# Order of the first loads, a layer norm over latents with its statistics as rows, and two tiles turned ahead of the expert stage's first product

## Time and profile before

| | |
|---|---|
| Median of 3 timed runs | 3268.74 us (3267.42 to 3273.45) |
| Profiled execution, own time | 3266.73 us |
| Its span, first to last instruction | 3264.7 us |
| PE busy | 2824.3 us, 87% |
| DVE, ACT, POOL busy | 57%, 49%, 21% |
| Granted TensorE clock, mean | 0.924 of full speed |

### The profile page before, as it was taken

One profiled execution on the slowest core, in us unless ns is written; L12 is line 12 of the kernel. 1 busy time (PEld: TensorE's weight loads), 2 busy tenths in 40 slices (PEclk: granted clock), 3 DMA queues, 4 the chain that ended last, 5 costly groups with the idle time before them and its releaser, 6 DMA issues. The chain is left out here.

```text
span 3264.7 us, 53416 instructions
## 1 busy us (share of the span) xinstructions
PE 2824.3 (87%) x18536; PEld 1728.8 (53%) x18537; DVE 1866.7 (57%) x4567; ACT 1584.1 (49%) x4331; POOL 678.6 (21%) x756
## 2 busy tenths in 40 slices
PE   7778988659999998679889999999988879959993
PEld 4635653425555555346555553455633455659992
DVE  5645765548787775758566642266423547743334
ACT  5425963227777774851246432154421539813331
POOL 3120021112112110112036520066300003301113
PEclk9878999679999999889999999999999989969996
DMA  1000020200000001000010010000000000141112
GB/s 71 3 15 5 2 85 0 71 0 1 2 2 1 2 2 63 1 14 2 17 41 1 1 64 0 7 1 1 1 29 13 7 23 2 79 170 37 35 33 83
DMA packets 36130, 80.64 MB, mean 25 GB/s; under 512 B 9089, under 2 KB 24530, under 8 KB 32050
## 3 DMA queue, kind: packets, MB, share of 16 engines
q1 hardware_dynamic: 30962, 64.68, 5.5%
q0 software_dynamic: 4368, 11.93, 1.3%
q10 hardware_dynamic: 560, 0.93, 0.1%
HBM read 63.18 MB, written 14.02 MB: 24 GB/s over the span
## 5 line engine op out<-in xcount | busy, mean ns | idle before, releaser
L2562 ACT ACTIVATE scores<-scores,min 128x128 f32<-128x128 f32 (+7 forms) x256 | 198.5, 775 | 86.7 <-DVE min L2545 82.6
L2543 DVE TENSOR_SCALAR zero_marks<-psum 128x128 f32<-128x128 f32 (+7 forms) x256 | 192.1, 750 | 67.8 <-PE psum L2475 65.9
L2545 DVE CUSTOM_DVE_ANT_0 scores<-psum,zero_marks 128x128 f32<-128x128 f32 (+7 forms) x256 | 194.1, 758 | 29.9 <-issue 0.9
L2482 PE MATMUL psum<-ident,scores 128*128 128x128 f32 x1152 | 172.9, 277 | 16.6 <-ACT probsT L2579 13.7
L2579 ACT ACTIVATE probsT<-psum 128x128 f32<-128x128 f32 (+7 forms) x256 | 163.0, 637 | 32.1 <-PE psum L2482 31.6
L4006 PE MATMUL psum<-Hn,W 128*128 128x512 f32 x384 | 169.9, 606 | 7.6 <-PEq L54 7.6
L1701 ACT ACTIVATE XT<-psum,early_weights 128x128 f32<-128x128 f32 x312 | 89.0, 368 | 176.2 <-PE psum L1621 176.2
L1621 PE MATMUL psum<-early_weights,XT 128*128 128x128 f32 x1248 | 150.8, 280 | 6.1 <-issue 3.2
L2482 PEld LDWEIGHTS psum<-ident,scores 128*128 128x128 f32 x1152 | 123.3, 141 | 55.9 <-issue 30.3
L1621 PEld LDWEIGHTS psum<-early_weights,XT 128*128 128x128 f32 x1248 | 145.9, 195 | 13.0 <-issue 11.9
L3854 POOL TENSOR_TENSOR probs<-probs,stat 128x512 f32<-128x512 f32 (+1 forms) x128 | 123.2, 986 | 99.6 <-DVE stat L3818 97.0
(11 more groups left out here) (628 smaller groups left out, 6728.5 us busy)
## 6 DMA issues: line engine op xcount, KB each, us to landing
W<-in_L3f_W SPq DMA_DIRECT2D x16, 1024.0 KB, 13.1
L3f_y_rows<-early_weights SPq DMA_DIRECT2D x39, 128.0 KB, 1.7
early_weights<-in_L2f_Wqkv SPq DMA_DIRECT2D x2, 1536.0 KB
W<-in_L2f_W SPq DMA_DIRECT2D x2, 1536.0 KB
XT<-in_xT SPq DMA_DIRECT2D x1, 2048.0 KB, 10.1
Xtok<-in_xtok SPq DMA_DIRECT2D x1, 2048.0 KB
L0f_rows<-Xtok SPq DMA_DIRECT2D x4, 512.0 KB, 2.9
W<-in_L0f_W SPq DMA_DIRECT2D x2, 1024.0 KB
```

The costliest lines, as they stand in the source:

```text
L2482: ins = pe.transpose(turned[:, kt * P:(kt + 1) * P], Sc[:, i % ROT, kt * P:(kt + 1) * P], K.ident[:])
L2543: dve.tensor_scalar(zero[:, i % 2, 0:n], sc(i)[:, 0:n], 0.0, -NEG, ALU.is_equal, ALU.mult)
L2545: dve.tensor_tensor_reduce(Sc[:, i % ROT, 0:n], sc(i)[:, 0:n], zero[:, i % 2, 0:n], 1.0, -NEG, ALU.add, ALU.min, low[:, i % ROT:i % ROT + ...
L2562: act.activation(p, p, ACT.Exp, bias=low[:, i % ROT:i % ROT + 1], scale=-1.0, accum_out=sums[:, u % 2, h:h + 1]).then_inc(s["exp_done"], 1)
```

## The change

Four places are edited.

1. In `setup`, SP waits for x and the first weights ahead of issuing the context and the token-major x, no longer behind it, and ACT issues its three loads in reverse order (cw, Wb, W).
2. `feature_ln` is replaced by `latent_ln`, with its statistics as rows: all 4 means first, then the sums of squares of both groups and all blocks into 8 rows of one bank, one root and one reciprocal on 8 x 512 values, then 4 products that spread the rows back over the partitions. The latents are worked on in place. POOL prepares two small matrices and clears a buffer in the same phase. It takes nine semaphores, the old one seven.
3. In the expert stage TensorE turns tile 1 ahead of up 0, and DVE does weights 0 ahead of x_out 0. The loop is the same.
4. In `L0_ffn` the phase of `block_mean` is gone; POOL's next phase begins with a memset of J to 1/128.

```diff
         @block.sync
         def _(sp):
             sp.dma_start(K.XT[0][:], w["xT"]).then_inc(s["loaded"], 16)
+            sp.wait_ge(s["loaded"], 16 * (1 + len(K.ahead)))
             sp.dma_start(K.ctxT[:], w["ctxT"]).then_inc(K.late, 16)
             sp.dma_start(K.Xtok[:], w["xtok"]).then_inc(K.late, 16)
-            sp.wait_ge(s["loaded"], 16 * (1 + len(K.ahead)))
...
-            for dst, src in K.ahead:
+            for dst, src in K.ahead[::-1]:
                 act.dma_start(dst, src).then_inc(s["loaded"], 16)
...
                 turn_x(0, 0)
+                turn_x(0, 1)
                 up(0, 0)
-                turn_x(0, 1)
...
-                x_out(0, 0)
                 dve.wait_ge(weights_in, 16 * (2 * EXPERTS + 1))
                 weights(0, 0)
+                x_out(0, 0)
                 x_out(0, 1)
                 weights(0, 1)
...
+def latent_ln(nc, K, J, src, g, b):
+    GROUPS_ = P // LAT
+    R = NB * GROUPS_
...
+        @block.gpsimd
+        def _(pool):
+            pool.memset(std[:], 0.0).then_inc(s["prepared"], 1)
+            pool.memset(wide[:], 0.0).then_inc(s["prepared"], 1)
+            pool.wait_ge(s["prepared"], 2)
+            pool.tensor_copy(wide[:, GROUPS_ * (NB - 1):GROUPS_ * NB], J.rearrange("p (g d) -> p g d", g=GROUPS_)[:, :, 0]).then_inc(s["prepared"], 1)
+            pool.tensor_copy(pick[:].rearrange("p j (g d) -> p (j g) d", g=GROUPS_), inner(K.ident[:, 0:R], LAT)).then_inc(s["prepared"], 1)
         @block.tensor
         def _(pe):
+            for j in range(NB):
+                pe.matmul(K.bank[j][:], J, src(j), start=True, stop=True).then_inc(s["mean_done"], 1)
+            pe.wait_ge(s["prepared"], 4)
+            for j in range(NB):
                 pe.wait_ge(s["squared"], j + 1)
+                at = GROUPS_ * (NB - 1 - j)
+                pe.matmul(K.bank[4][0:R, :], wide[:, at:at + R], sq[:, j % 2, :], start=(j == 0), stop=(j == NB - 1)).then_inc(s["var_done"], 1)
+            pe.wait_ge(s["recip_done"], 1)
+            for j in range(NB):
+                pe.wait_ge(s["centred"], j + 1)
+                pe.matmul(K.bank[j][:], pick[:, j, :], std[:], start=True, stop=True).then_inc(s["spread"], 1)
         @block.vector
         def _(dve):
+            for j in range(NB):
                 dve.wait_ge(s["mean_done"], j + 1)
+                dve.tensor_tensor(src(j), src(j), K.bank[j][:], ALU.subtract).then_inc(s["centred"], 1)
+            dve.wait_ge(s["std_done"], 1)
+            dve.reciprocal(std[0:R, :], std[0:R, :]).then_inc(s["recip_done"], 1)
+            for j in range(NB):
+                dve.wait_ge(s["spread"], j + 1)
+                dve.tensor_tensor(src(j), src(j), K.bank[j][:], ALU.mult).then_inc(s["normed"], 1)
         @block.scalar
         def _(act):
+            for j in range(NB):
                 act.wait_ge(s["centred"], j + 1)
                 if j >= 2:
                     act.wait_ge(s["var_done"], j - 1)
+                act.activation(sq[:, j % 2, :], src(j), ACT.Square).then_inc(s["squared"], 1)
+            act.wait_ge(s["var_done"], NB)
+            act.wait_ge(s["prepared"], 1)
+            act.activation(std[0:R, :], K.bank[4][0:R, :], ACT.Sqrt, bias=K.eps[0:R, 0:1]).then_inc(s["std_done"], 1)
+            for j in range(NB):
                 act.wait_ge(s["normed"], j + 1)
+                act.activation(src(j), src(j), ACT.Identity, scale=g, bias=b)
...
-                feature_ln(nc, K, J[:], NB, 1, lambda j, h: cb(j), lambda j, h: cb(j), lambda j: g[:], lambda j: b[:])
+                latent_ln(nc, K, J[:], cb, g[:], b[:])
...
-            block_mean(nc, K, J[:], P)
...
                 @block.gpsimd
                 def _(pool):
+                    pool.memset(J[:], 1.0 / P)
                     pool.iota(ordi[:], pattern=[[1, PICKED]], base=1, channel_multiplier=0).then_inc(s["counted"], 1)
```

More of the change, by code:

```diff
@@ L2160, in _ @@
             pool.affine_select(out=v, in_=v, compare_op=ALU.is_ge, fill=0.0, base=size - 1, pattern=[[size, n], [0, size]], channel_multiplier=-1)
[L2163 to L2169, removed]
+def latent_ln(nc, K, J, src, g, b):
+    GROUPS_ = P // LAT
+    R = NB * GROUPS_
+    names = "prepared mean_done centred squared var_done std_done recip_done spread normed"
+    with ExitStack() as es, phase(nc, K.sems, names) as (block, s):
+        sq = sbuf(es, nc, "squares", [P, 2, BLK])
+        std = sbuf(es, nc, "std", [P, BLK])
+        wide = sbuf(es, nc, "averaging_columns", [P, (2 * NB - 1) * GROUPS_])
+        pick = sbuf(es, nc, "row_picks", [P, NB, P])
+        @block.gpsimd
[5 more added lines that the diff above has]
+            pool.tensor_copy(pick[:].rearrange("p j (g d) -> p (j g) d", g=GROUPS_), inner(K.ident[:, 0:R], LAT)).then_inc(s["prepared"], 1)
@@ L2171, in _ @@
         @block.tensor
         def _(pe):
[L2173 to L2182, removed]
-                pe.wait_ge(s["squared"], j + 1)
[L2184 to L2188, removed]
+            for j in range(NB):
+                pe.matmul(K.bank[j][:], J, src(j), start=True, stop=True).then_inc(s["mean_done"], 1)
@@ L2190, in _ @@
         @block.vector
         def _(dve):
-            def centre(j):
+            for j in range(NB):
                 dve.wait_ge(s["mean_done"], j + 1)
[L2194 to L2208, removed]
+                dve.tensor_tensor(src(j), src(j), K.bank[j][:], ALU.subtract).then_inc(s["centred"], 1)
@@ L2210, in _ @@
+            dve.wait_ge(s["std_done"], 1)
[3 more added lines that the diff above has]
+                dve.tensor_tensor(src(j), src(j), K.bank[j][:], ALU.mult).then_inc(s["normed"], 1)
         @block.scalar
         def _(act):
-            def square(j):
+            for j in range(NB):
                 act.wait_ge(s["centred"], j + 1)
@@ L2215, in square @@
                     act.wait_ge(s["var_done"], j - 1)
[L2216 to L2222, removed]
-                act.wait_ge(s["var_done"], j + 1)
-                if j >= 2:
-                    act.wait_ge(s["normed"], j - 1)
-                act.activation(std[:, j % 2, :], K.bank[2 + j % 2][:], ACT.Sqrt, bias=K.eps[:, 0:1]).then_inc(s["std_done"], 1)
+                act.activation(sq[:, j % 2, :], src(j), ACT.Square).then_inc(s["squared"], 1)
[3 more added lines that the diff above has]
+            for j in range(NB):
                 act.wait_ge(s["normed"], j + 1)
-                for h in range(halves_):
-                    ins = act.activation(dst(j, h), xc[:, j % 2, h, :], ACT.Identity, scale=g(j)[:, h:h + 1], bias=b(j)[:, h:h + 1])
-                ins.then_inc(s["out"], 1)
+                act.activation(src(j), src(j), ACT.Identity, scale=g, bias=b)
 def feature_ln_rows(nc, K, J, n, halves_, src, dst, g, b, late=()):
```

## The result

The changed kernel took **3246.78 us** in the median of 4 runs (3245.30 to 3250.36), against 3268.62 for the kernel before on the same occasion (3267.42 to 3273.45). The ratio is 0.9932, interval 0.9918 to 0.9945: 21.8 us less, where 18.9 were forecast. The span of the profiled execution fell from 3264.7 to 3243.3 us, that is by 21.4; the mean granted clock rose from 0.924 to 0.928.

A forecast was written before the change was run, and what follows sets the result against it. The prediction took one chain of barrier-closed phases to bound the kernel, so the last-ending wait counts at each place. Gains 5.5 + 1.25 + 8.7 + 3.45 = 18.9 us off 3268.7 gave 3249.8, range 3241 to 3257.

The forecast's parts named there:

- Opening: Setup: with context and token-major x held back, the last needed landing comes at 10.7 and TensorE starts 5.5 us earlier.
- Rival (b): Opening not bound by bytes: last weights land when they did and the late issues cost 0.9 us; 3256.2, chance 0.06.
- J: Ahead of L0_ffn's products: the phase in which only POOL works goes whole, gain 1.25 us (1.0 to 1.3).
- Latent layer norm: Layer norm of the latents: 29.95 us become 21.25 with one reciprocal replacing four, gain 8.7 us.
- rival (c): More gain than forecast: faster spreads, second tile wholly, query product no longer cold (-1.7), earlier landing; 3243.9, chance 0.11.
- Rival (a): New layer norm: the clock doesn't rise and products run at 1.2 GHz, +5.4 us, second tile +0.5; 3255.7, chance 0.12.
- Expert stage: Start of the expert stage: earlier first product, shorter wait before the second tile and higher clock, gain 3.45 us (2.55 to 4.45).
- The head: Start of the expert stage: first product could start at 2906.5 instead of 2908.32, 1.8 us earlier, less 0.5.
- the contact: Expert stage: DVE's weight copy runs beside POOL's gather issues, costing 0.5 us (bounds nothing and 0.9).
- The gap: Between first and second expert tile: 3.1 us shrink to the weight copy and two hand-overs, 1.45; 1.65 gained.
- The clock: Second expert tile's products: 1.0 us came from the lower clock after the old wait; half, 0.5, counted as gain.
- (d): Expert loop: weight copies and gather issues collide in every one of 39 tiles, +37.4 at worst; 3287, chance 0.03.

The follow-up runs named there:

- the old order: The changed kernel with ACT's three first loads put back to W, Wb, cw: 3248.40 us, ratio 0.9929 to the kernel before.
- filled wait: The changed kernel with four more products into a free bank while TensorE waits for the latent layer norm's reciprocal: 3245.11 us, ratio 0.9922.
- the repetition: The changed kernel run again unaltered, on another chip, against the kernel before: 3248.74 us, ratio 0.9928.
- the place above: The changed kernel with semaphores cleared after 55 names instead of 100, where one new clear precedes the query product's second group: 3256.15 us, ratio 0.9966.

## Why the prediction was right, step by step

The forecast was 3249.8 us with 3241 to 3257; measured 3246.8 and, again, 3248.7. The mechanism held at each of its four places, and the gain came out 2 to 3 us larger. That the sum fits so well is partly luck: two of its terms move by 1 to 4 us from one execution to the next.

**Opening (forecast 5.5, measured 5.2).** The estimate of the last landing was 10.7, it was 11.06, and the queue was the one named: not x, but the W behind it. Issues (0.81 for 0.9) and hand-over (0.45 for 0.44) as read. Rival (b), that the opening isn't bound by bytes, is refuted: holding back the 2.6 MB (2560 KB; the prediction calls them 2.5) brought every landing to 11.06 or before, in the old order to 11.36, though not to 9.5, where the bytes alone would end.

**J (1.25, measured 1.24).** As read off.

**Latent layer norm (8.7, measured 7.7 in it and 1.6 behind it).** In the first trace means and squares' products took 659.81 - 649.55 = 10.3 us instead of 8.9: I had let two products run at the lower level, as in rows 7, but all four means nearly did (6.64 us for their eight instructions). The transfer from L0_ffn's layer norm was good: 6.32 us from first spread to fourth multiplication, 6.56 forecast. The reciprocal of 8 rows took 3.34, as that of 13 and of 128. The term left out of the forecast was the query product: with only 1.87 us of stillness ahead of it, not 10.4, it ran at the upper level, 7.10 for 8.73. It stood in rival (c) with 1.7. Rival (a), all products at 1.2 GHz, is refuted: the squares' eight instructions took 3.69 us, the four means at 0.50 6.64, and the granted clock was 1.00 from 657 to 661. These sizes are one execution's. From the first mean to the last scale-and-shift the eight traces without a filled wait took 18.4 to 22.3 us, around the 21.25 of the forecast; in all of them the query product took 7.10 or 7.11. So this term was right in kind, and its size depends on where the clock's level falls.

**Expert stage (3.45, measured 4.9; 4.1 in the repetition).** The head: 1.3 forecast (1.8 less 0.5 for the contact), 1.7 measured. VectorE's weight copy does lie over the second gather's issue, from 2884.55 to 2885.80, and stretches it from 0.96 to 1.38: 0.42, within the bounds of nothing and 0.9. The Trainium skill (SBUF — State Buffer, "Who interferes with whom") would have the two exclude each other for the whole instruction. For the whole of the issue the trace does not agree: then it would have ended at 2885.80 + 0.95 = 2886.75 and not at 2885.92, or the copy would have been late, which took 1.25 us as against 1.23 elsewhere. But the issue ended 0.12 us behind the copy, and 0.11 to 0.13 behind it in all nine traces with this order, as if its last part alone had to wait for the whole copy; that reading is not tested. The gap: 1.6 for 1.65. The clock: 1.63 measured where I counted half of 1.0. The term that was mis-sized is the price of the lower level on the second tile: 1.0 came from the mean clock over 3.4 us, while the 32 products took 5.46 us and then 3.83; and at a gap of 1.50 the clock stayed up. In the repetition the first tile gave 0.8 us of that back (5.99 for 5.17), so that both tiles together gained 0.8, which lies near the forecast's 0.5. The second tile's 1.63 is therefore sure only together with the first tile's time.

**The sum, and the rivals.** In the first pair of traces too high by 0.3 (opening) and 1.0 (layer norm proper), too low by 1.6 (query product) and 1.4 (expert stage): 1.7 net, and 0.7 came from elsewhere. So the total profited from errors of either sign. Of rival (c)'s four terms two came, the query product and the second tile. The other side, (d), collisions in all the loop's tiles, did not happen: from the third turn to its last product's end the loop took 277.9 to 278.2 us in all fourteen traces, of either order. The 2 us lost up to the end are lost behind it. A clear of the semaphores, costed at 1.0 wherever it stands, cost more where it brought down the clock (2.9 us at the place above).

## What to carry to other kernels

Where small weights and large tensors load together, look which landing ends the wait, and issue nothing large that isn't needed until it has come; put its issue behind the barrier that it would delay. In a layer norm over partitions take the statistics as rows, so that one reciprocal serves all blocks, and give TensorE something to do while it waits for it: four products on ones turned 5.4 to 6.3 us of spreads into 3.7. Count a shortened gap not by its length alone but by what the products behind it cost at the lower clock, and take that price from several traces: the same gap did not always bring it.

## What I had not expected of the hardware

- A load of 12 KB landed 15.4 us after its issue beside 5.5 MB of other loads. With 2.6 MB of these held back it took 9.6 us when issued last, 7.3 when issued first.
- The length of a wait didn't settle the clock behind it. Stillness of 1.50 us ahead of the second tile was followed by products at 2.4 GHz (3.83 us) in each of nine traces, and 1.87 us ahead of the query product by 7.10 or 7.11 us at the upper level in each trace of the new layer norm. But 2.9 us ahead of the second tile was followed by 5.46, 5.46, 5.46, 5.17 and once 3.83, and 3.01 us ahead of the means by anything from 6.67 to 3.67. The wait of 4.14 us ahead of the spreads was followed by a slower group in each trace without fillers (5.40 to 6.30 us for 3.70).
- The kernel before took 3255.2 us on one chip and 3268.6 to 3271.6 on the other occasions, and on the first the parts' times add up to less than their rows. Some 7 to 10 us of that lie behind the expert stage's last product. A gain of 0.1% can be read in rows where no median shows it.
